# Top-k threshold search: first two bits by constant trials, scores loaded before the hand-over, small work moved between rounds

## The reference, cut to what matters

```python
n = b * t                                   # 8192 tokens
capacity = max(1, int(CAPACITY_FACTOR * n / e))   # e = 8 experts: 1024
scores = (x_flat @ Wg.T).T                  # 8 x 8192
top_vals, token_idx = jax.lax.top_k(scores, capacity)
token_w = jax.nn.softmax(top_vals, axis=-1)
xg = x_flat[token_idx]
```

## Time and profile before

| | us |
|---|---|
| median of 3 runs | 3260.74 |
| lowest and highest of them | 3258.59 and 3265.33 |
| the profiled execution, its own time | 3246.65 |
| the profiled execution's span | 3244.8 |
| busy in the span: PE, DVE, ACT, POOL | 2716.3, 2264.2, 1767.0, 2083.2 |

### The profile page before, as it was taken

How to read it: one execution, slowest core, us unless ns; L and a number is a source line. 1 busy time by engine, 2 the same in 40 slices (tenths; PEclk the granted TensorE clock), 3 DMA queues, 4 the chain that set the end, 5 groups by cost and what they waited for, 6 DMA issues and landing times.

```text
span 3244.8 us, 44912 instructions
## 1 busy us (share of the span) xinstructions
PE 2716.3 (84%) x15742; PEld 1461.3 (45%) x15742; DVE 2264.2 (70%) x2386; ACT 1767.0 (54%) x3106; POOL 2083.2 (64%) x1301
## 2 busy tenths in 40 slices
PE   7788878887888788877855599996999999479998
PEld 3233233333333233333323366564767676445565
DVE  3999999999999999999997522212767676532211
ACT  4777778778777778778762122223444443022221
POOL 3899999999999999999894054443333333034453
PEclk9889889888999888988976699998999999679999
DMA  5556655664565655665562033332111111213442
GB/s 142 123 121 141 148 136 128 141 159 124 139 144 137 147 134 123 142 160 125 129 136 75 14 87 75 82 59 57 40 54 47 54 47 41 69 43 80 89 92 26
DMA packets 225469, 325.27 MB, mean 100 GB/s; under 512 B 40705, under 2 KB 116993, under 8 KB 225122
## 3 DMA queue, kind: packets, MB, share of 16 engines
q1 hardware_dynamic: 200674, 288.32, 36.0%
q0 software_dynamic: 24576, 34.10, 6.3%
HBM read 236.34 MB, written 85.98 MB: 99 GB/s over the span
## 4 chain that ended last, share of the span: by engine, by line
PE 52%; DVE 20%; issue 8%; POOL 7%; ACT 6%; DMA 5%; SPq 1%; DVEq 0%; POOLq 0%; ACTq 0%
PE m_wk L912 9%; PE t_wb L2267 9%; PE g_h L1536 7%; PE f_h L1536 7%; DVE m_pair L789 6%; DVE m_hc L789 4%; DMA m_bc<-bcd 4%; PE m_y L1009 4%; DVE m_hc L798 4%; PE g_yp L1550 3%; PE f_yp L1550 3%; POOL m_side L698 3%; POOL m_hc L707 2%; PE t_num L2267 2%; PE t_a_ps L2267 2%
## 5 line engine op out<-in xcount | busy, mean ns | idle before, releaser
L698 POOL TENSOR_TENSOR m_side<-m_du_r,m_bc 128x1024 f32<-128x1024 f32 x384 | 900.9, 2361 | 9.7 <-DMA m_du_r<-ddd 9.7
L707 POOL TENSOR_TENSOR m_hc<-m_hc,m_bc 128x1024 f32<-128x1024 f32 x224 | 527.6, 2358 | 117.6 <-DVE m_hc L789 117.3
L434 ACT ACTIVATE m_pair<-m_delta_r,m_a_neg 128x512 f32<-128x512 f32 x768 | 497.8, 680 | 179.8 <-DVE m_hc L798 93.8
L789 DVE TENSOR_TENSOR_SCAN m_pair<-m_pair,m_side 128x1024 f32<-128x1024 f32 x224 | 511.5, 2283 | 20.3 <-ACT m_pair L434 17.0
L1009 PE MATMUL m_y<-m_hc,m_fold 128*32 128x512 f32 x2048 | 324.6, 709 | 202.2 <-DVE m_hc L798 143.8
L789 DVE TENSOR_TENSOR_SCAN m_hc<-m_pair,m_side 128x1024 f32<-128x1024 f32 x160 | 362.9, 2277 | 10.5 <-POOL m_side L698 10.5
L798 DVE TENSOR_TENSOR m_hc<-m_pair,m_bc 128x1024 f32<-128x1024 f32 x288 | 350.7, 1218 | 5.7
L912 PE MATMUL m_wk<-m_xnT,m_w_in 128*128 128x512 f32 x488 | 295.5, 737 | 23.6 <-DVE m_delta L774 23.6
L912 PE MATMUL m_wk<-m_xs,m_cw_diag 128*128 128x512 f32 x480 | 226.8, 605 | 10.1 <-ACT m_xs L504 10.1
L1536 PE MATMUL g_h<-g_xgT,g_w 128*128 128x512 f32 x512 | 224.2, 598 | 0.8 <-ACT g_xgT L1430 0.8
L1536 PE MATMUL f_h<-f_xgT,f_w 128*128 128x512 f32 x512 | 223.5, 596 | 0.8 <-ACT f_xgT L1430 0.8
(11 more groups left out here) (338 smaller groups left out, 4966.6 us busy)
## 6 DMA issues: line engine op xcount, KB each, us to landing
m_delta_r<-ddd SPq DMA_DIRECT2D x252, 256.0 KB, 6.7
m_du_r<-ddd SPq DMA_DIRECT2D x252, 256.0 KB, 7.6
m_bc<-bcd SPq DMA_DIRECT2D x192, 128.0 KB, 3.0
ddd<-m_delta SPq DMA_DIRECT2D x31, 512.0 KB, 3.0
ddd<-m_du SPq DMA_DIRECT2D x31, 512.0 KB, 3.8
f_w<-in_w SPq DMA_DIRECT2D x24, 512.0 KB, 6.2
g_w<-in_w SPq DMA_DIRECT2D x24, 512.0 KB, 6.0
m_xt<-in_x SPq DMA_DIRECT2D x16, 512.0 KB, 9.9
```

The costliest lines, as they stand in the source:

```text
L434: last = nc.scalar.activation(to, delta_r[:, c % 2, q, :], ACT.Exp, scale=a_neg[:, c * NQ + q, st:st + 1])
L698: nc.gpsimd.tensor_tensor(side[:, un % RING, :, :], du_r[:, c % 2, 2 * h:2 * h + 2, :], bc[:, 0, st:st + 1, :].to_broadcast([P, 2, T]), AL ...
L707: nc.gpsimd.tensor_tensor(hc[:, un % RING, :, :], hc[:, un % RING, :, :], bc[:, 1, st:st + 1, :].to_broadcast([P, 2, T]), ALU.mult).then_i ...
L789: nc.vector.tensor_tensor_scan(to, decay, added, 0.0, ALU.mult, ALU.add).then_inc(S["scan"], 1)
```

## The change

1. SP loads the first 15 sequences' scores (8 DMAs of 15 rows), `blk`, `step`, `ident` and the three later constants before it stores the last sequence's results, in the epilogue of `mamba` and of `attention` (`early`). The tile `unit` is gone.
2. The last sequence's scores go from SBUF straight into rows 15, 31, ... of `sc`, two of the four DMAs issued by SP and two by ACT; `done` waits for them as well.
3. `one` and `blk_b` are made at the end of the stage before, ahead of DVE's wait for `done` (`constants`).
4. The two counts that gave the first two bits are replaced by one round like the others, with three constant thresholds `FIRST`; its number is turned into two masks of bits (`sign`, `bit30`) and the first trials.
5. The row maxima are taken in round 1, the maxima of the experts in rounds 3 and 4, their negative in round 6, and PE transposes the row maxima after round 1, spreads the maxima after round 4 and transposes the exponentials after round 7.

The core of the diff:

```diff
+    FIRST = (-(2.0 - 2.0 ** -23), 0.0, 2.0)
...
+        def early(sp):
+            for e in range(NE):
+                sp.dma_start(sc[e * NB:e * NB + NB - 1, :],
+                             scores[e, 0:(NB - 1) * T].rearrange("(b t) -> b t", t=T)).then_inc(S["ld_sc"], 16)
+            sp.dma_start(blk[:], w["blk"]).then_inc(S["ld_b"], 16)
+            for tile, src in consts:
+                sp.dma_start(tile[:], src).then_inc(S["ld"], 16)
+            for tile, src in later:
+                sp.dma_start(tile[:], src).then_inc(S["ldc"], 16)
+
+        last_scores = [sc[NB - 1:P:NB, j * P:(j + 1) * P] for j in range(TJ)]
+        def constants(dve):
+            nc.vector.memset(one[:], 1.0).then_inc(S["one"], 1)
+            dve.wait_ge(S["ld_b"], 16)
+            nc.vector.tensor_copy(blk_b[:], blk[:]).then_inc(S["one"], 1)
+
+        search = Search(early, last_scores, S["ld_sc"], 16 * (NE + TJ), constants)
...
-            sp.dma_start(sc[:], scores.rearrange("e (b t) -> (e b) t", t=T)).then_inc(S["ld_sc"], 16)
-            sp.dma_start(blk[:], w["blk"]).then_inc(S["ld_b"], 16)
-            for tile, src in consts:
-                sp.dma_start(tile[:], src).then_inc(S["ld"], 16)
-            for tile, src in later:
-                sp.dma_start(tile[:], src).then_inc(S["ldc"], 16)
...
+            dve.wait_ge(S["ld_sc"], search.all_landed)
+            masks(FIRST)
+            holding(0)
+            bits = num[:].bitcast(I32)
+            V.tensor_scalar(sign[:], bits, 30, 31, ALU.logical_shift_left, ALU.arith_shift_right).then_inc(S["found"], 1)
+            V.tensor_scalar(bit30[:], bits, 30, 1 << 30, ALU.logical_shift_left, ALU.bitwise_and)\
+                .then_inc(S["found"], 1)
+            dve.wait_ge(S["ld"], loaded)
+            dve.wait_ge(S["found"], 2)
+            V.scalar_tensor_tensor(trial[:], steps(0), bit30[:, 0:1], sign[:].to_broadcast([P, PAIR + 1]),
+                                   ALU.bitwise_xor, ALU.bitwise_xor).then_inc(S["trial"], 1)
+            for r in range(1, ROUNDS + 1):
+                dve.wait_ge(S["trial"], r)
+                masks([trial[:, v:v + 1].bitcast(F32) for v in range(PAIR)])
+                V.tensor_tensor(pre[:], steps(r), trial[:, PAIR:PAIR + 1].to_broadcast([P, PAIR + 1]),
+                                ALU.bitwise_xor).then_inc(S["found"], 1)
+                if r == 1:
+                    V.tensor_reduce(rmax[:], sc[:], AX.X, ALU.max).then_inc(S["rmax"], 1)
...
+                holding(r)
...
             def epilogue():
+                sp_.wait_ge(S["st_sc"], (NB - 1) * TJ * 16)
+                sp_.wait_ge(S["iz"], NB * 4)
+                search.early(sp_)
                 store_x1(NB - 1)
                 store_xn1(NB - 1)
-                store_sc(NB - 1)
+                sp_.wait_ge(S["scev"], NB)
+                for j in range(TJ // 2):
+                    sp_.dma_start(search.last_scores[j], sc[j * SB:j * SB + NE, :]).then_inc(search.landed, 16)
...
                 sc_out(NB - 1)
+                act.wait_ge(S["scev"], NB)
+                for j in range(TJ // 2, TJ):
+                    act.dma_start(search.last_scores[j], sc[j * SB:j * SB + NE, :]).then_inc(search.landed, 16)
```

More of the change, by code:

```diff
@@ L137 @@
 Stage = namedtuple("Stage", "scope sync gpsimd scalar tensor vector")
+Search = namedtuple("Search", "early last_scores landed all_landed constants")
 def turns(n, prologue, body, epilogue):
@@ L1250, in moe @@
         sc = s.sb("sc", [P, T])
+        one = s.sb("one", [P, T])
         blk = s.sb("blk", [P, P])
@@ L1566, in totals_of, with maxima_row, maxima_column, exponentials @@
                 last.then_inc(S["tot"], 1)
[L1568 to L1580, removed]
+            def maxima_row():
+                pe.wait_ge(S["ld"], loaded)
+                pe.wait_ge(S["rmax"], 1)
+                nc.tensor.transpose(mrow[0:1, 0:P], rmax[:], ident[:]).then_inc(S["mrow"], 1)
+            def maxima_column():
+                pe.wait_ge(S["emb"], 1)
+                nc.tensor.matmul(mcol[:, 0:1], emax_b[:, :, :].rearrange("p e b -> p (e b)"), one[0:1, 0:1],
+                                 start=True, stop=True).then_inc(S["mcol"], 1)
+            def exponentials():
+                pe.wait_ge(S["ex"], 1)
+                for j in range(TJ):
+                    last = nc.tensor.transpose(texp[:, j * P:(j + 1) * P], ex[:, j * P:(j + 1) * P], ident[:])
+                last.then_inc(S["ext"], 1)
             pe.wait_ge(S["one"], 2)
-            for r in range(ROUNDS):
+            for r in range(ROUNDS + 1):
                 totals_of(r)
-            pe.wait_ge(S["above"], ROUNDS * PAIR + 2)
+                if r == 1:
+                    maxima_row()
+                if r == 4:
+                    maxima_column()
+                if r == 7:
+                    exponentials()
+            pe.wait_ge(S["above"], (ROUNDS + 1) * PAIR + 2)
             nc.tensor.matmul(tot[:, 0:1], blk[:], cg[:], start=True, stop=True).then_inc(S["tot"], 1)
@@ L1704, in vector @@
-            dve.wait_ge(S["mcol"], 1)
-            V.tensor_scalar(nmax[:], mcol[:, 0:1], -1.0, None, ALU.mult).then_inc(S["nmax"], 1)
-            for r in range(ROUNDS):
-                count_round(r)
-            dve.wait_ge(S["trial"], ROUNDS + 2)
+            dve.wait_ge(S["trial"], ROUNDS + 1)
             thr = trial[:, PAIR:PAIR + 1].bitcast(F32)
@@ L1901, in epilogue @@
             def epilogue():
+                sp.wait_ge(S["st_sc"], (NB - 1) * TJ * 16)
+                sp.wait_ge(S["qk"], NB * 4)
+                sp.wait_ge(S["v"], NB * 2)
+                search.early(sp)
                 store(NB - 1, (NB - 1) % 2)
@@ L1904, in epilogue @@
                     sp.wait_ge(S[n], NB * 16)
-                sp.wait_ge(S["st_sc"], NB * TJ * 16)
+                sp.wait_ge(search.landed, search.all_landed)
                 sp.sem_inc(done, 1)
@@ L2116, in epilogue @@
                 sc_out(NB - 1)
+                act.wait_ge(S["scev"], NB)
+                for j in range(TJ // 2, TJ):
+                    act.dma_start(search.last_scores[j], sc[j * Q:j * Q + NE, :]).then_inc(search.landed, 16)
             turns(NB, prologue, body, epilogue)
@@ L2615, in program @@
         f.scope.release()
-        g = moe(nc, done, "g", xn3, out, sc3, a, by_pool, 1, cleared)
+        g, g_search = moe(nc, done, "g", xn3, out, sc3, a, by_pool, 1, cleared)
         t.scope.release()
```

116 lines of the change are left out of this document (47 added, 69 removed).

## The result

The changed kernel takes **3253.64 us** (median of 22 runs, 3251.34 to 3256.36). The kernel before, run beside it on the same chip, takes 3260.32 us (22 runs, 3256.79 to 3265.33). The ratio is 0.9980, with a 95% interval of 0.9973 to 0.9986: 6.5 us less, and 4.6 to 8.8 us by the interval.

What follows compares the result with a forecast made beforehand. Bound by serial waits at both hand-overs and alternating DVE and PE in the rounds. Gains of 5.55 and 5.4 us, together 11.0, less 7.0 for POOL, gave 4.0 us: 3260.74 to 3256.7 us, range 3248.0 to 3261.0.

Steps and rivals of the forecast that it cites:

- only the IOTA holds it up: Rival, round 0 of each search: the CAST gets in only after the third mask; gain 7.0 us, time 3253.7, chance 0.20.
- The hand-over: From last scores to DVE's first mask, after mamba and attention: DVE starts 3.5 and 3.3 us earlier.
- The first two bits: Start of each search: round 0 takes 3.2 us where the counts took 3.9, saving 0.7 us.
- The first trial round: Round after the first two bits in each search: 4.24 us becomes 2.89, saving 1.35 us.
- POOL beside the masks: Round 0 of each search: POOL's IOTA and CAST hold up DVE's masks, giving back 3.5 us a search, 7.0 in all.
- the CAST, asking from 1762.96, gets in between masks: Round 0, first search: POOL's CAST runs 1763.2 to 1765.1 between masks, so masks 1 and 2 end at 1765.9.
- What is laid between rounds costs nothing: DVE's 0.69 us and PE's 1.43 us holes between rounds: maxima and exponentials fit there, cost 0.
- The early loads: End of mamba and attention: 14 issues, 6.3 us, ahead of SP's last stores; one store 4.2 us later, cost 0.
- The slower rival: End of attention: early loads hold up the last stores; at 1.8 us an issue 11.6 us slower, 3272.3, chance 0.05.
- The first rival: Round 0 of each search: POOL does not hold up DVE; gain 11.0 us, time 3249.7, chance 0.30.

Runs made afterwards that it cites:

- POOL in the holes: The changed kernel with POOL's IOTA and CAST halved, each half started after a round's third mask: 3233.09 us, before 3245.64 us, ratio 0.9964.

## Why the prediction was right or wrong

**The time.** 3253.64 us lies in the range of 3248.0 to 3261.0. The forecast, 4.0 us less, had the direction; the change gave 6.5, at the edge of what I had called telling it from none (0.2%). It lies below the forecast's own range of 3254.5 to 3259, at the price of the rival "only the IOTA holds it up", 3253.7, which also has nearly the mechanism. By the steps of the forecast:

* **The hand-over, 3.5 and 3.3 us forecast: too large.** It gave 2.33 in the first search. In the second DVE starts at 2788.03, 2.89 us after ACT's first issue, against 2787.26 - 2782.11 = 5.15 before: 2.26. The term mis-sized is the price of a score DMA: I carried over the 0.34 us step and the 1.22 us landing of a DMA to DRAM. To `f_sc` and `g_sc` in SBUF the issues took 0.6 to 1.2 us and the landing 1.66 and 2.02. I had written that neither was in any row and then taken the lower bound's side; the landing was within the range that I left for it (1.22 to 2.9), the issue was not costed at all.
* **The first two bits, 0.7 us: right** where POOL is away. Round 0 takes 3.21 us with POOL in the holes, forecast 3.2. **The first trial round, 1.35: right**, 2.89 us.
* **POOL beside the masks, 3.5 us back a search: right in kind, too large in size.** DVE does wait for the whole of a long POOL instruction, which no row of before had shown. It cost 1.7 us. The step that failed is the second half, "the CAST, asking from 1762.96, gets in between masks": POOL did not come first but DVE, by 0.04 us, so mask 0 was out before the IOTA, the masks were all but over when the CAST started (0.2 us were left), and it fell into DVE's wait for PE. The IOTA I had at 1.85; it cost mask 1 1.76 (2207 ns against 446).
* The Trainium skill, page "SBUF — State Buffer", section "Who interferes with whom", has a DVE instruction in a two-port mode and a GpSimd instruction exclude each other for the whole of an instruction. The runs agree: 2207 ns against 446 for a mask, with one IOTA beside it.
* That the total came within 2.5 us is luck, since the two errors had opposite signs: 2.2 us too much gain for the two hand-overs, and 3.6 us too much loss to POOL in the two searches. The forecast was 4.0; with both terms as measured it is 4.6 + 1.4 + 2.7 - 3.4 = 5.3, which is what the traces show (5.4). The runs give 6.5 with an interval from 4.6; whether the 1.1 between them is real, and where it would lie, is open.
* **What is laid between rounds costs nothing: right.** Round 1 is as long as any other, and behind the exponentials PE has 0.53 us left. **The early loads: right.** The late store was forecast 4.2 us later and moved so; it lands before the last scores are issued. The slower rival had no part: the eight loads of `g_sc` took 3.44 us, 0.43 an issue, where it needed over 1.44.
* **The first rival** (DVE is not held up, 11.0 us) is refuted: masks of 2.2 us.

Each search needs POOL's numbers only long after the rounds. The change took away the wait that had kept masks and POOL apart (the first masks came at 1768.31, when both long instructions were over the earlier trace rows), and nothing in it kept them apart in its place.

## What to carry to other kernels

When a load or a wait at the head of a stage is taken away, ask what starts at the same release on the other engines: work that was hidden in the old wait may now stand beside the critical instructions, and if the two exclude each other, the gain is given back by just that instruction's length. Moving it away wholesale may only move the collision (the version with POOL behind the rounds lost 1.4 us there); cut into pieces that fit the critical engine's own waits, and begun by the event that opens such a wait, it cost nothing here (round 0 in 3.21 us). And price a DMA by rows with the same destination: source and shape alone missed a factor of two.

## What the runs showed of the hardware

**DVE waits for POOL in several forms, and not in all.** Beside the long IOTA of POOL a mask (one SBUF input, fp32) took 2.21 us in place of 0.45. Beside the long CAST a SCALAR_TENSOR_TENSOR of two SBUF inputs and 512 columns took 2.19 in place of 0.75, a CAST of 128 columns 1.28 in place of 0.16, a COPY of 128 elements 1.28 in place of 0.21. A counting pass over 512 columns kept its 0.69 beside the IOTA and its 0.74 beside the CAST. With POOL behind the rounds, DVE's scan of two SBUF inputs (TENSOR_TENSOR_SCAN, at 1807.42) kept its 1.28 us beside the IOTA, which ran until 1808.22. The one that comes second waits: the IOTA, second by 0.04 us, took 2.23 in place of 1.95.

**The last scores' DMAs cost more into SBUF rows than into DRAM.** Issues of 4 KB from the same source took 0.56 us and more each to every 16th partition of `f_sc`, 0.3 to DRAM, and landed 1.66 against 1.22 us after their start. ACT's first issue of the program took 1.16 us, its later ones 0.57 to 0.61. What in the destination costs this, and whether the 1.16 has to do with SP's issue beside it, was not tried.

**Behind the exponentials in PE's hole its clock rose in some searches.** There two rounds are 0.25 us shorter each. In the kernel with POOL in the holes, the windows over the first search (us, busy of each engine, and the granted clock ahead of the last two numbers) and a row of PE's timeline:

```profile
1782.00:1785.00 3.00, 2.48 (x35) 2.08 (x33) 2.20 (x10) 0.59 (x1) 0.00 (x0) 0.50 0.00 0
1785.00:1788.00 3.00, 1.57 (x36) 1.19 (x34) 2.46 (x10) 0.00 (x0) 0.00 (x0) 0.99 0.60 42
```

```profile
1787.21 1.20 PE L1593 MATMUL f_yp<-f_junk,f_blk_b 128*128 128x64 bf16 x24 [1.43 <-DVE f_junk L1693]
```

PE had been busy for 2.48 of 3 us, with the transposes between two rounds' totals, and then ran at its 2.4 GHz level for some 3 us. The totals took 1.20 in place of 1.46 us. In the changed kernel's own profile the same transposes left the clock at its 1.2 GHz level in both searches, in the second with PE just as busy:

```profile
2812.00:2815.00 3.00, 2.48 (x34) 2.08 (x31) 2.10 (x8) 0.59 (x1) 0.00 (x0) 0.50 0.06 4
2815.00:2818.00 3.00, 1.57 (x28) 1.33 (x25) 2.09 (x8) 0.00 (x0) 0.00 (x0) 0.50 0.77 57
```

One execution can do both: with POOL behind the rounds the first search takes 49.08 us from its first issue to `f_gt`, with the totals at 1.20 us, and the second 49.52, with all of them at 1.46. It is worth 0.5 us where it happens; what decides it was not tried.
